# Swin-style block on one core: the first layer norm moved from channels on partitions to tokens on partitions

## The chip, the cores and the metric

One core of one Trainium2 chip. The metric is the device time of one execution in microseconds. Before the change the median of 3 runs is 596.34 us (595.48 to 596.77).

## What is computed

The input `x` is 32 images of 96 channels by 16 x 16 tokens, in float32. Two layers follow each other. Only the start of the first one is touched:

```python
x = x.transpose(0, 2, 3, 1)                       # tokens x 96 channels
mu = x.mean(-1, keepdims=True)                    # layer norm over the 96 channels of a token
var = ((x - mu) ** 2).mean(-1, keepdims=True)
xn = (x - mu) * rsqrt(var + 1e-5) * norm1_g + norm1_b
xs = roll(xn, (-4, -4))                           # windows of 8 x 8 tokens, 4 per image
q, k, v = split(xw @ qkv_w + qkv_b)               # 12 heads of 8 channels
attn = softmax(q @ k.T * SCALE + rel_bias + mask)
x = x + roll(attn @ v @ proj_w + proj_b, (4, 4))
x = x + gelu(layernorm2(x) @ fc1_w + fc1_b) @ fc2_w + fc2_b
```

The second layer (a layer norm over the whole image, depthwise convolutions, attention between channels) is not touched.

## The kernel before, in words

Three stages run one after the other: window attention with the first residual (`window_attention`), the MLP (`mlp`) and the channel attention. The whole activation lives in SBUF as `stream`, 96 channels on partitions by 32 x 256 tokens.

Window attention is written out by hand for each engine. Each engine has a function `step(t, ...)` that says in which order it does its parts of the work, and runs it for t = -3 to 32 (`led_image_loop`, L62). Engines take their instructions in order, so a wait of one instruction holds everything behind it on that engine. The work is software pipelined over images. Step t does the attention of image t, the projection of image t - 1, the second scores of t + 1, the q, k and v of image t + 2, and the first layer norm of image t + 3. An image has two pairs of windows, so most operations of the attention come twice a step (p = 0 and 1).

The first layer norm keeps channels on partitions. TensorE multiplies the image by the matrix `center` (`centre`, L517), ScalarE squares the result (L338), TensorE averages the squares with the matrix `average` (`spread`, L522), ScalarE makes the inverse deviation by a logarithm and an exponential (`inverse_deviation`, L344 and L347, 96 x 256 elements each), and VectorE multiplies while it puts the tokens into window order (`normalise`, L424, two instructions).

TensorE's order in a step (L590) is: turn the probabilities of (t, 0) (L561); project t - 1 (L588); scores of (t + 1, 1) (L551); weigh (t, 0) (L574); centre t + 3 (L517); turn (t, 1); turn the heads of (t, 0) (L583); q, k and v of t + 2 (L529, L531, L537); weigh (t, 1); spread t + 3 (L522); scores of (t + 2, 0); turn the heads of (t, 1). All are float32.

ScalarE's order (L384) is: copy_ot of (t - 1, 1) (L379); copy_turned (t, 0) (L374); exponent (t, 1) (L368); square t + 3; copy_turned (t, 1); copy_ot (t, 0); copy_q t + 2 (L354); exponent (t + 1, 0); copy_v t + 2 (L363, four instructions, which wait for weigh (t, 1)); inverse_deviation t + 3. VectorE's order (L468) is: residual t - 1 (L465); normalise t + 2; add_bias (t + 1, 1) (L441); weigh_heads (t, 0) (L456 and L459); find_peak (t + 1, 1) (L449); copy_k t + 2 (L430); weigh_heads (t, 1); add_bias and find_peak (t + 2, 0). GpSimd subtracts the peaks (L324).

Two waits tie ScalarE to TensorE at the end of a step:

```python
def project(t, par):
    pe.wait_ge(s["ot_copied"], (t + 1) * 2)          # copy_ot of image t, both pairs
    pe.wait_ge(s["v_copied"], up_to(t + 2) * 4)      # copy_v of image t + 2
```

SyncE's queue issues all loads: image 0, constants, images 1 to 3 (`LOADS`, L280 and L281, into `stream`), then images 4 to 31 as two large transfers, then 34 small loads of weights for the later stages (L296).

Of the kernel before, what the change touches and what calls it, by code (L numbers as in the profile page):

```python
# [21 lines left out]
N = H * W  # L22
# [24 lines left out]
LOADS = ((0, 1), (1, 1), (2, 1), (3, 1), (4, B - 4))  # L47
UNROLLED = 4
# [13 lines left out]
def led_image_loop(engine, step):  # L62

    step(-3, 1)
    step(-2, 0)
    step(-1, 1)
    image_loop(engine, lambda t, half, par: step(t, par), tail=2)
    step(B, 0)
# [119 lines left out]
def window_attention(nc, ctx, a, sem, stream, ident, center, average, w_late, weights_in, zeroed_final):  # L188
# [3 lines left out]
    def bank(name, count=1):  # L192
# [15 lines left out]
    squares = sb("squares", [C, N])  # L208
    log_var = sb("log_var", [C, N])
    eps = sb("eps", [C, 1])  # L210
    rstd = sb("rstd", [C, N])
# [17 lines left out]
    centred = ps_a[0:C, 0, 0:N]  # L229
    ps_var = ps_a[0:C, 0, N:2 * N]  # L230
# [8 lines left out]
    normalising_in = sem("normalising_in")  # L239
# [4 lines left out]
    pe_set = sem("pe_set")  # L244
    zeroed = sem("zeroed")
    x_landed = [sem(f"x_landed{k}") for k in range(len(LOADS))]
    s = {n: sem(n) for n in (
        "centred_ready", "squares_ready", "var_ready", "log_ready", "rstd_ready", "normed_ready",
# [4 lines left out]
    FIRST, SECOND = 7, 7  # L253
# [4 lines left out]
    @block.sync  # L258
    def _(sp):
        def column(name):  # L260
            return a[name].rearrange("(c a) -> c a", a=1)

        normalising = ((center[:, :], a["c_center"]), (average[:, :], a["c_average"]))
        first = ((w_in[:, :], a["L0_conv_qkv_w"]),
                 (cols[:, 0:1], column("L0_conv_norm1_g")), (cols[:, 1:2], column("L0_conv_norm1_b")),
                 *((cols[:, 2 + k:3 + k], a["L0_conv_qkv_b"][k * C:(k + 1) * C].rearrange("(c a) -> c a", a=1))
                   for k in range(3)),
                 (head_mask[:, :], a["c_head_mask"]))
        second = (*((shift_mask[WN * top:WN * (top + 1), left, :], a["c_shift_mask"][WN * left:WN * (left + 1), top])
                    for top in range(2) for left in range(2)), (ident[:, :], a["c_ident"]),  # L270
                  (w_proj[:, :], a["L0_conv_proj_w"]), (cols[:, 5:6], column("L0_conv_proj_b")))
        assert (len(first), len(second)) == (FIRST, SECOND)
        late = weight_loads(a, w_late)

        def load(k):

            t, count = LOADS[k]
            images = x[t:t + count].rearrange("b c h w -> c b (h w)")
            rows = stream[:, t * N:(t + count) * N].rearrange("p (b n) -> p b n", n=N)
            sp.dma_start(rows[:, :, 0:N - SS * W], images[:, :, SS * W:N]).then_inc(x_landed[k], 16)  # L280
            sp.dma_start(rows[:, :, N - SS * W:N], images[:, :, 0:SS * W]).then_inc(x_landed[k], 16)  # L281

        load(0)
        for dst, src in normalising:
            sp.dma_start(dst, src).then_inc(normalising_in, 16)
# [12 lines left out]

    @block.gpsimd
    def _(pool):  # L300


        table = a["L0_conv_rel_bias"]
# [7 lines left out]
        nc.gpsimd.memset(eps[:, :], EPS).then_inc(zeroed, 1)  # L311
        nc.gpsimd.memset(v_blocks[:, :, :, :, :, :, :], 0.0).then_inc(zeroed, 1)
        pool.wait_ge(zeroed, 2)
        for e in range(2):
            for par in range(2):
                nc.gpsimd.memset(v_blocks[64 * e:64 * e + 64, par, :, :, :, e, HD:VC], 1.0).then_inc(zeroed, 1)
        pool.wait_ge(zeroed, 6)
        nc.gpsimd.memset(w_late["final"][:, :], 0.0).then_inc(zeroed_final, 1)

        def subtract_peak(t, p, par):  # L320
            u = t * 2 + p
            pool.wait_ge(s["peak_ready"], u + 1)
            sc = scores[:, par, p, :].rearrange("p (h m) -> p h m", m=WN)
            nc.gpsimd.tensor_tensor(sc, sc, peak[:, par, p, :].unsqueeze(2).to_broadcast((128, HEADS, WN)),  # L324
                                    ALU.subtract).then_inc(s["shifted"], 1)

        def step(t, half, par):
            subtract_peak(t, 0, par)
            subtract_peak(t, 1, par)

        image_loop(pool, step)

    @block.scalar
    def _(act):
        def square(t):
            act.wait_ge(s["centred_ready"], t + 1)
            need(act, s["var_ready"], t)
            nc.scalar.activation(squares[:, :], centred, ACT.Square).then_inc(s["squares_ready"], 1)  # L338

        def inverse_deviation(t):  # L340

            act.wait_ge(s["var_ready"], t + 1)
            need(act, s["rstd_ready"], t)
            nc.scalar.activation(log_var[:, :], ps_var, ACT.Ln, bias=eps[:, 0:1]).then_inc(s["log_ready"], 1)  # L344
            act.wait_ge(s["log_ready"], t + 1)
            need(act, s["normed_ready"], t * PAIRS)
            nc.scalar.activation(rstd[:, :], log_var[:, :], ACT.Exp, scale=-0.5).then_inc(s["rstd_ready"], 1)  # L347

# [7 lines left out]
        def copy_v(t, par):  # L356
            act.wait_ge(s["v_ready"], t + 1)
# [24 lines left out]
        act.wait_ge(zeroed, 6)  # L382

        def step(t, par):  # L384
# [5 lines left out]
            if real(t + 3):  # L390
                square(t + 3)
# [15 lines left out]
    def _(dve):  # L407
# [12 lines left out]
        def normalise(t):  # L420
            dve.wait_ge(s["rstd_ready"], t + 1)
            need(dve, s["v_ready"], t)
            for p in range(PAIRS):
                nc.vector.tensor_tensor(window_rows(normed[:, p * 2 * WN:(p + 1) * 2 * WN], p), shifted(centred, p),  # L424
                                        shifted(rstd[:, :], p), ALU.mult).then_inc(s["normed_ready"], 1)
# [36 lines left out]
        def add_residual(t):  # L462
            dve.wait_ge(s["proj_ready"], t + 1)
# [4 lines left out]
        def step(t, par):  # L468
# [19 lines left out]
        nc.vector.tensor_scalar(w_qkv[:, :], w_in[:, :], cols[:, 0:1], None, ALU.mult).then_inc(set_up, 1)  # L488
# [5 lines left out]
        nc.vector.tensor_scalar(b_q[:, :], b_q[:, :], SCALE, None, ALU.mult).then_inc(set_up, 1)  # L494
        led_image_loop(dve, step)

    @block.tensor
    def _(pe):
# [13 lines left out]
        def centre(t):  # L512
            for k, (first, count) in enumerate(LOADS):
                if is_image(t, min(first, UNROLLED)):
                    pe.wait_ge(x_landed[k], 32)
            need(pe, s["normed_ready"], t * PAIRS)
            nc.tensor.matmul(centred, center[:, :], stream[:, bass.ds(t * N, N)],  # L517
                             start=True, stop=True).then_inc(s["centred_ready"], 1)

        def spread(t):  # L520
            pe.wait_ge(s["squares_ready"], t + 1)
            nc.tensor.matmul(ps_var, average[:, :], squares[:, :], start=True, stop=True).then_inc(s["var_ready"], 1)  # L522

        def make_q_and_k(t):
            if is_image(t, 0):
                pe.wait_ge(set_up, 1)
# [63 lines left out]
        def step(t, par):  # L590
            if real(t):
                turn(t, 0, par)
            if real(t - 1):
# [5 lines left out]
            if real(t + 3):  # L599
                centre(t + 3)  # L600
            if is_image(t, -3):
                fold_q_k_v()
            if real(t):
                turn(t, 1, par)
                turn_heads(t, 0)
            if real(t + 2):
# [4 lines left out]
            if real(t + 3):  # L611
                spread(t + 3)
# [7 lines left out]
        pe.wait_ge(normalising_in, 16 * 2)  # L620
# [660 lines left out]
```

## Time and profile before

| | |
|---|---|
| median of 3 runs | 596.34 us |
| the profiled execution's own time | 599.53 us |
| its span, first to last instruction | 597.8 us |
| TensorE (PE) busy | 548.4 us, 92% |
| VectorE (DVE) busy | 362.9 us, 61% |
| ScalarE (ACT) busy | 327.9 us, 55% |
| GpSimd (POOL) busy | 161.2 us, 27% |
| window attention / MLP / channel attention | up to about 289 / 405 / 598 us |

Times in the timeline are microseconds from the span's start. The span is cut from one profiled execution, 1.7 us shorter than that execution's own time, which in turn lies 3.2 us above the median. PE is TensorE's matmuls, PEld its weight loads, which overlap the matmuls. Matmul ends are modelled, so two neighbouring matmul groups can overlap by some tenths of a microsecond; distances from start to start are the firmer measure. One float32 matmul appears as two records, a transposition as one.

### The profile page before, as it was taken

The page shows a single profiled execution, that of the slowest core. Times are in us where ns is not written, and L with a number is a line of the kernel's source. Part 1 is how long each engine was busy: PE and PEld are TensorE (multiplying, and loading weights), DVE is VectorE, ACT ScalarE, POOL GpSimd, SP SyncE. Part 2 cuts the span into 40 slices and gives each one's busy share as a digit, 9 for nine tenths or more (in the row PEclk, how much of TensorE's full clock was granted, in tenths as well). Part 3 has the DMA queues.
Part 4 walks back from the last instruction along what each step waited for, and adds up shares of the span by engine and source line. Part 5 has one row for each costly group of instructions (what it writes and reads, how often), then busy time and mean ns, then how long its engine had stood idle before and what let it go on. Part 6 is the DMA issues. An engine that isn't in the chain of part 4 may idle for free. (4 is left out here: it accounts for less than half of the span.)

```text
span 597.8 us, 20839 instructions
## 1 busy us (share of the span) xinstructions
PE 548.4 (92%) x7900; PEld 327.6 (55%) x7900; DVE 362.9 (61%) x839; ACT 327.9 (55%) x749; POOL 161.2 (27%) x198
## 2 busy tenths in 40 slices
PE   2799999999999999998799999992899999999997
PEld 1466676666676666666333444441345555555563
DVE  0768778787778888787274333336325666655544
ACT  1367777777777777776499443332323444444432
POOL 7123333333333333333000000003322333333310
PEclk9999999999999999999799999996558999999999
DMA  4900000000000000000000000002432444444421
GB/s 86 206 7 3 1 0 0 0 0 0 0 0 0 0 0 0 0 0 2 2 0 0 0 0 0 0 0 49 108 87 78 115 111 114 113 115 115 125 63 29
DMA packets 28059, 22.87 MB, mean 38 GB/s; under 512 B 12280, under 2 KB 26744, under 8 KB 28024
## 3 DMA queue, kind: packets, MB, share of 16 engines
q1 hardware_dynamic: 24440, 16.66, 11.5%
q0 software_dynamic: 3584, 5.72, 4.2%
q8 instruction: 25, 0.41, 0.3%
q14 instruction: 10, 0.08, 0.1%
HBM read 15.22 MB, written 7.13 MB: 37 GB/s over the span
## 5 line engine op out<-in xcount | busy, mean ns | idle before, releaser
L324 POOL TENSOR_TENSOR scores<-scores,peak 128x768 f32<-128x768 f32 x64 | 94.3, 1474 | 174.0 <-DVE peak L449 174.0
L896 POOL DMA_DIRECT2D x_stack<-padded_x x96 | 52.3, 547 | 109.6 <-PE ps_v L1163 87.2
L441 DVE TENSOR_TENSOR scores<-ps_scores,bias 128x768 f32<-128x768 f32 x64 | 60.9, 951 | 25.0 <-PE ps_scores L551 25.0
L449 DVE TENSOR_REDUCE peak<-scores 128x12 f32<-128x768 f32 x64 | 60.7, 948 | 1.1
L574 PE MATMUL ps_out<-v_blocks,probs_t 128*64 128x54 f32 x1536 | 58.9, 227 | 2.1 <-ACT out_t L379 1.6
L574 PEld LDWEIGHTS ps_out<-v_blocks,probs_t 128*64 128x64 f32 x1536 | 50.6, 139 | 18.0 <-issue 15.2
L1163 PE MATMUL ps_qk<-x_stack,conv_w 40*32 40x256 f32 x1536 | 54.0, 411 | 5.5 <-ACT final_w L1009 5.5
L374 ACT COPY probs_t<-ps_probs 128x768 f32<-128x768 f32 x64 | 51.1, 798 | 13.4 <-PE ps_probs L561 13.4
L747 ACT ACTIVATE hidden<-ps_hidden,fc_b_folded 128x512 f32<-128x512 f32 x48 | 32.4, 688 | 42.9 <-PE ps_hidden L700 42.7
L430 DVE SCALAR_TENSOR_TENSOR k_blocks<-ps_scores,b_k,head_mask 96x1024 f32<-96x1024 f32 x32 | 41.0, 1280 | 23.5 <-PE ps_scores L531 23.5
L368 ACT ACTIVATE scores<-scores 128x768 f32<-128x768 f32 x64 | 54.1, 845 | 0.0
L1163 PE MATMUL ps_v<-x_stack,conv_w 40*32 40x256 f32 x1536 | 54.0, 411 | 0.0
L561 PE MATMUL ps_probs<-ident,scores 128*128 128x128 f32 x384 | 53.7, 277 | 0.0
L561 PEld LDWEIGHTS ps_probs<-ident,scores 128*128 128x128 f32 x384 | 45.5, 143 | 4.8 <-issue 1.0
L551 PE MATMUL ps_scores<-k_blocks,q_sb 32*64 32x256 f32 x768 | 45.0, 415 | 2.9 <-DVE scores L441 2.7
L782 DVE SCALAR_TENSOR_TENSOR mixed<-ps_y,fc_b,stream 96x384 f32 (+3 forms) x32 | 13.9, 476 | 54.1 <-PE ps_y L707 54.1
L338 ACT ACTIVATE squares<-ps_a 96x256 f32<-96x256 f32 x32 | 12.2, 381 | 60.9 <-PE ps_a L517 50.8
L700 PE MATMUL ps_hidden<-mixed,fc_scaled 96*128 (+1 forms) x96 | 43.7, 592 | 0.0
L707 PE MATMUL ps_y<-hidden,fc 128*96 128x512 f32 x96 | 43.7, 592 | 0.0
L1163 PEld LDWEIGHTS ps_qk<-x_stack,conv_w 40*32 40x32 f32 x1536 | 27.3, 112 | 28.3 <-issue 16.1
L981 ACT COPY qk_sb<-ps_qk 128x512 f32<-128x512 f32 x32 | 18.8, 586 | 40.1 <-PE ps_qk L1163 40.1
L363 ACT COPY v_blocks<-ps_b 64x96 f32<-64x96 f32 x128 | 30.7, 240 | 11.2 <-PE ps_out L574 7.3
(123 smaller groups left out, 857.2 us busy)
## 6 DMA issues: line engine op xcount, KB each, us to landing
x_stack<-padded_x SPq DMA_DIRECT2D x96, 54.0 KB
x_stack<-padded_x POOLq DMA_DIRECT2D x96, 54.0 KB, 2.7
padded_x<-x_pad SPq DMA_DIRECT2D x32, 121.5 KB, 2.5
out<-y_sb SPq DMA_DIRECT2D x32, 96.0 KB, 2.0
stream<-in_x SPq DMA_DIRECT2D x1, 2016.0 KB, 12.6
stream<-in_x SPq DMA_DIRECT2D x1, 672.0 KB, 16.0
rel_rows<-in_L_conv_rel_bias POOLq DMA_DIRECT2D x16, 24.0 KB, 2.4
stream<-in_x SPq DMA_DIRECT2D x4, 72.0 KB, 2.0
```

The source lines that it names most:

```text
L324: nc.gpsimd.tensor_tensor(sc, sc, peak[:, par, p, :].unsqueeze(2).to_broadcast((128, HEADS, WN)), ALU.subtract).then_inc(s["shifted"], 1)
L368: nc.scalar.activation(scores[:, par, p, :], scores[:, par, p, :], ACT.Exp).then_inc(s["probs_ready"], 1)
L374: nc.scalar.copy(probs_t[:, :], ps_turned).then_inc(s["turned_copied"], 1)
L441: nc.vector.tensor_tensor(scores[:, par, p, :].rearrange("p (g c) -> p g c", g=NG), ps_scores[:, :, 0:GROUP * WN], bias[:, p, :].rearrange ...
L449: nc.vector.tensor_reduce(peak[:, par, p, :], scores[:, par, p, :].rearrange("p (h m) -> p h m", m=WN), AX_X, ALU.max).then_inc(s["peak_re ...
L551: mm = nc.tensor.matmul(ps_scores[64 * w:64 * w + 64, g, 0:GROUP * WN], q, k, start=True, stop=True, skip_group_check=True)
L561: mm = nc.tensor.transpose(ps_turned[:, q * 128:(q + 1) * 128], scores[:, par, p, q * 128:(q + 1) * 128], ident[:, :])
L574: mm = nc.tensor.matmul(ps_out[64 * top:64 * top + 64, 0, q * 2 * VC:(q + 3) * 2 * VC], probs_t[:, q * 128 + 64 * top:q * 128 + 64 * top + ...
L700: nc.tensor.matmul(ps_hidden[:, par * HT + h, :], fc1[:, h * 128:(h + 1) * 128], mixed[:, bass.ds(k * CHUNK, CHUNK)], start=True, stop=Tru ...
L707: mm = nc.tensor.matmul(ps_y[0:C, par, :], w["fc2"][:, h, :], hidden[:, par, h, :], start=(h == 0), stop=(h == HT - 1))
L896: engine.dma_start(x_stack[64 * half + i * HC:64 * half + (i + 1) * HC, slot, :, :], rows).then_inc(landed[slot], 16)
L1163: mm = nc.tensor.matmul(ps[32 * k:32 * k + 32, r, :], conv_w[rows, kind, j, k, :], grid(x_stack[rows, slot, k, :], PADW)[:, :, j:j + W], s ...
```

## The change

The layer norm of image t + 3 is done with tokens on partitions. A step now holds: `turn_tokens`, two transpositions of an image half (96 x 128) into 128 tokens x 96 channels in PSUM; `measure`, two statistics instructions on VectorE (128 x 96 each), and `gather_spread`, two aggregations (128 x 6 to 128 x 2); `inverse_deviation`, the same logarithm and exponential over 128 x 2; `scale`, two ScalarE copies (128 x 96) with the inverse deviation as a per-partition scale; `turn_back`, two transpositions to channels x tokens, in the next step; `copy_normed`, two ScalarE copies into window order. The mean is no longer subtracted from the data: `center` is multiplied once into the weights (`fold_mean`). The images are loaded a second time, one by one, into a two-slot buffer `x_now`; `stream` is loaded whole by two transfers, and is first used by the residual.

Core of the diff:

```diff
@@ SyncE @@
-        load(0)
+        def load(t, par):
+            need(sp, s["tokens_ready"], t - 1)
+            image = x[bass.ds(t, 1)].rearrange("a c h w -> c (a h w)")
+            sp.dma_start(x_now[:, par, 0:N - SS * W], image[:, SS * W:N]).then_inc(x_now_in[par], 16)
+            sp.dma_start(x_now[:, par, N - SS * W:N], image[:, 0:SS * W]).then_inc(x_now_in[par], 16)
+        load(0, 0)
+        sp.dma_start(ident[:, :], a["c_ident"]).then_inc(turning_in, 16)
         for dst, src in first:
             sp.dma_start(dst, src).then_inc(consts_in, 16)
-        load(1)
+        load(1, 1)
         for dst, src in second:
             sp.dma_start(dst, src).then_inc(second_in, 16)
-        for k in range(2, len(LOADS)):
-            load(k)
+        load(2, 0)
+        load_stream()
+        load(3, 1)
         sp.wait_ge(zeroed_final, 1)
         for dst, src in late:
             sp.dma_start(dst, src).then_inc(weights_in, 16)
+        image_loop(sp, lambda t, half, par: load(t, par), lead=2, start=4)
@@ ScalarE @@
+        def scale(t):
+            act.wait_ge(s["rstd_ready"], t + 1)
+            need(act, s["turned_back"], t)
+            for h in range(2):
+                nc.scalar.activation(scaled[:, h, :], ps_tokens[:, h, :], ACT.Copy,
+                                     scale=rstd[:, h:h + 1]).then_inc(s["scaled_ready"], 1)
+        def copy_normed(t):
+            act.wait_ge(s["turned_back"], t + 1)
+            need(act, s["v_ready"], t)
+            for p in range(PAIRS):
+                nc.scalar.copy(window_rows(normed[:, p * 2 * WN:(p + 1) * 2 * WN], p),
+                               shifted(ps_scaled, p)).then_inc(s["normed_ready"], 1)
@@ ScalarE's step @@
                 exponent(t, 1, par)
-            if real(t + 3):
-                square(t + 3)
+            if real(t + 2):
+                copy_normed(t + 2)
...
                 exponent(t + 1, 0, 1 - par)
+            if real(t + 3):
+                inverse_deviation(t + 3)
+                scale(t + 3)
             if real(t + 2):
                 copy_v(t + 2, par)
-            if real(t + 3):
-                inverse_deviation(t + 3)
@@ VectorE's step @@
                 add_residual(t - 1)
-            if real(t + 2):
-                normalise(t + 2)
...
                 find_peak(t + 1, 1, 1 - par)
+            if real(t + 3):
+                measure(t + 3)
+            if real(t + 3):
+                await_stats(t + 3)
             if real(t + 2):
                 copy_k(t + 2)
+            if real(t + 3):
+                gather_spread()
             if real(t):
                 weigh_heads(t, 1)
@@ TensorE @@
+        def fold_mean():
+            pe.wait_ge(set_up, 1)
+            nc.tensor.matmul(ps_folded, center[:, :], w_gained[:, :], start=True, stop=True).then_inc(folded, 1)
+        def turn_tokens(t, half, par):
+            pe.wait_ge(x_now_in[par], (half + 1) * 32)
+            need(pe, s["scaled_ready"], t * 2)
             need(pe, s["normed_ready"], t * PAIRS)
+            for h in range(2):
+                mm = nc.tensor.transpose(ps_tokens[:, h, :], x_now[:, par, h * 128:(h + 1) * 128], ident[0:C, 0:C])
+            mm.then_inc(s["tokens_ready"], 1)
+        def turn_back(t):
+            pe.wait_ge(s["scaled_ready"], (t + 1) * 2)
+            for h in range(2):
+                mm = nc.tensor.transpose(ps_scaled[:, h * 128:(h + 1) * 128], scaled[:, h, :], ident[:, :])
+            mm.then_inc(s["turned_back"], 1)
@@ TensorE's step @@
                 turn(t, 0, par)
+            if real(t + 2):
+                turn_back(t + 2)
             if real(t - 1):
                 project(t - 1, 1 - par)
...
                 weigh(t, 0, par)
-            if real(t + 3):
-                centre(t + 3)
             if real(t):
                 turn(t, 1, par)
                 turn_heads(t, 0)
+            if real(t + 3):
+                turn_tokens(t + 3, half + 1 + par, 1 - par)
             if real(t + 2):
                 make_q_and_k(t + 2)
                 make_v(t + 2)
             if real(t):
                 weigh(t, 1, par)
-            if real(t + 3):
-                spread(t + 3)
             if real(t + 2):
                 score(t + 2, 0)
```

Besides, GpSimd sets `eps` before its loads of the bias table, ScalarE waits for that alone ahead of its first step and for the zeroed `v_blocks` only at its first copy_v, and the residual of image 0 waits for `stream`. VectorE copies the folded weights (96 x 288) out of PSUM ahead of its first step.

## Rows read from the trace of the kernel before

**Rows 1.** Waits over the whole span: total us, times, longest
```profile
PE ps_b L588 <- ACT out_t L379: 11.1, 30, 0.5
```

**Rows 2.** Timeline of one inner step: start us, us, engine, line, operation, idle before
```profile
120.23 0.67 PE L522 MATMUL ps_a<-squares,average 96*96 96x256 f32 x2
...
120.40 1.04 ACT L363 COPY v_blocks<-ps_b 64x96 f32<-64x96 f32 x4 [0.23 <-PE ps_out L574]
...
121.47 0.47 ACT L344 ACTIVATE log_var<-ps_a,eps 96x256 f32<-96x256 f32 x1
...
122.05 0.42 ACT L347 ACTIVATE rstd<-log_var 96x256 f32<-96x256 f32 x1
...
122.37 0.24 ACT L379 COPY out_t<-ps_out 96x128 f32<-96x128 f32 x1
...
122.75 0.67 PE L588 MATMUL ps_b<-out_t,w_proj 96*96 96x256 f32 x2 [0.34 <-ACT out_t L379]
...
123.95 0.91 PE L574 MATMUL ps_out<-v_blocks,probs_t 128*64 128x54 f32 x24
...
126.07 0.60 PE L529 MATMUL ps_scores<-normed,w_qkv 96*96 96x256 f32 x2
...
127.22 1.28 DVE L430 SCALAR_TENSOR_TENSOR k_blocks<-ps_scores,b_k,head_mask 96x1024 f32<-96x1024 f32 x1 [0.63 <-PE ps_scores L531]
```

**Rows 3.** Timeline, TensorE's projection of image 0 and of image 28
```profile
41.83 0.67 PE L588 MATMUL ps_b<-out_t,w_proj 96*96 96x256 f32 x2 [0.18 <-ACT out_t L379]
...
268.34 0.67 PE L588 MATMUL ps_b<-out_t,w_proj 96*96 96x256 f32 x2 [0.18 <-ACT out_t L379]
```

**Rows 4.** Timeline of step 29, which has no first layer norm in it
```profile
269.55 0.91 PE L574 MATMUL ps_out<-v_blocks,probs_t 128*64 128x54 f32 x24
...
270.39 0.87 PE L561 MATMUL ps_probs<-ident,scores 128*128 128x128 f32 x6
...
271.44 0.32 PE L583 MATMUL ps_out<-ident,heads_out 128*96 128x128 f32 x1 [0.17 <-DVE heads_out L459]
...
271.59 0.60 PE L529 MATMUL ps_scores<-normed,w_qkv 96*96 96x256 f32 x2
...
276.60 0.91 PE L574 MATMUL ps_out<-v_blocks,probs_t 128*64 128x54 f32 x24
```

**Rows 5.** Groups by line: busy us, mean ns of one, idle before
```profile
L786 DVE BATCH_NORM_STATS2 stats<-mixed (+1 forms) x32 | 12.0, 415 | 2.0 <-DVE mixed L782 1.0
...
L456 DVE RECIPROCAL recip<-ps_out 128x12 f32<-128x12 f32 x64 | 14.1, 221 | 4.8 <-PE ps_out L574 4.8
...
L990 ACT ACTIVATE logits<-logits 128x24 f32<-128x24 f32 x32 | 7.1, 223 | 8.6 <-DVE logits L1079 8.6
...
L379 ACT COPY out_t<-ps_out 96x128 f32<-96x128 f32 x64 | 16.5, 258 | 3.3 <-PE ps_out L583 3.2
```

**Rows 6.** Timeline of the start, TensorE and SyncE's queue
```profile
7.75 1.12 PE L503 MATMUL ps_out<-cols,w_in 96*96 96x1 f32 x6 [2.41 <-DMA head_mask<-in_c_head_mask]
...
13.39 4.30 SPq L281 DMA_DIRECT2D stream<-in_x  x1
...
16.41 1.06 PE L529 MATMUL ps_scores<-normed,w_qkv 96*96 96x256 f32 x2
...
17.74 8.40 SPq L296 DMA_DIRECT2D fc<-in_L_conv_fc_w  x2
...
37.93 3.23 SPq L296 DMA_DIRECT2D alpha<-in_L_conv_alpha  x8
...
45.16 0.60 PE L529 MATMUL ps_scores<-normed,w_qkv 96*96 96x256 f32 x2
```

**Rows 7.** Page, loads of one image: KB each, median us to landing
```profile
stream<-in_x SPq DMA_DIRECT2D x4, 72.0 KB, 2.0
```

**Rows 8.** Stretches: length, busy us of PE, PEld, DVE, ACT, POOL, granted clock
```profile
280.00:285.00 5.00, 3.56 (x51) 2.73 (x47) 1.46 (x5) 2.22 (x5) 0.83 (x1) 1.00 0.00 0
285.00:290.00 5.00, 2.49 (x28) 1.49 (x29) 1.39 (x4) 1.49 (x4) 0.10 (x1) 0.95 0.01 3
```

More of the change, by code:

```diff
@@ L62, in led_image_loop @@
 def led_image_loop(engine, step):
[L64 to L68, printed above, removed]
+    step(-3, -2, 1)
+    step(-2, -1, 0)
+    step(-1, -1, 1)
+    image_loop(engine, step, tail=2)
+    step(B, B // 2, 0)
 def image_loop(engine, step, tail=1, lead=1, between=None, start=0):
@@ L207, in window_attention @@
     b_proj = sb("b_proj", [C, 1])
[L208 to L211, printed above, removed]
+    w_gained = sb("w_gained", [C, 3 * C])
+    token_stats = sb("token_stats", [128, 2, 6])
+    spread = sb("spread", [128, 2, 2])
+    log_var = sb("log_var", [128, 2])
+    eps = sb("eps", [128, 1])
+    rstd = sb("rstd", [128, 2])
+    scaled = sb("scaled", [128, 2, C])
+    x_now = sb("x_now", [C, 2, N])
     normed = sb("normed", [C, N])
@@ L244, in window_attention @@
     pe_set = sem("pe_set")
+    folded = sem("folded")
+    centred = sem("centred")
     zeroed = sem("zeroed")
-    x_landed = [sem(f"x_landed{k}") for k in range(len(LOADS))]
+    x_now_in = [sem("x_now_in0"), sem("x_now_in1")]
+    stream_in = sem("stream_in")
     s = {n: sem(n) for n in (
-        "centred_ready", "squares_ready", "var_ready", "log_ready", "rstd_ready", "normed_ready",
+        "tokens_ready", "stats_ready", "spread_ready", "log_ready", "rstd_ready", "scaled_ready", "turned_back", "normed_ready",
         "q_ready", "k_ready", "q_copied", "k_copied", "v_ready", "v_copied",
@@ L261, in column @@
             return a[name].rearrange("(c a) -> c a", a=1)
-        normalising = ((center[:, :], a["c_center"]), (average[:, :], a["c_average"]))
-        first = ((w_in[:, :], a["L0_conv_qkv_w"]),
+        first = ((center[:, :], a["c_center"]), (w_in[:, :], a["L0_conv_qkv_w"]),
                  (cols[:, 0:1], column("L0_conv_norm1_g")), (cols[:, 1:2], column("L0_conv_norm1_b")),
@@ L269, in _ @@
         second = (*((shift_mask[WN * top:WN * (top + 1), left, :], a["c_shift_mask"][WN * left:WN * (left + 1), top])
-                    for top in range(2) for left in range(2)), (ident[:, :], a["c_ident"]),
+                    for top in range(2) for left in range(2)), (average[:, :], a["c_average"]),
                   (w_proj[:, :], a["L0_conv_proj_w"]), (cols[:, 5:6], column("L0_conv_proj_b")))
@@ L273, in _, with load_stream @@
         late = weight_loads(a, w_late)
[L275 to L281, printed above, removed]
-        load(0)
-        for dst, src in normalising:
-            sp.dma_start(dst, src).then_inc(normalising_in, 16)
+        def load(t, par):
[3 more added lines that the diff above has]
+            sp.dma_start(x_now[:, par, N - SS * W:N], image[:, 0:SS * W]).then_inc(x_now_in[par], 16)
+        def load_stream():
+            images = x.rearrange("b c h w -> c b (h w)")
+            rows = stream[:, :].rearrange("p (b n) -> p b n", n=N)
+            sp.dma_start(rows[:, :, 0:N - SS * W], images[:, :, SS * W:N]).then_inc(stream_in, 16)
+            sp.dma_start(rows[:, :, N - SS * W:N], images[:, :, 0:SS * W]).then_inc(stream_in, 16)
+        load(0, 0)
+        sp.dma_start(ident[:, :], a["c_ident"]).then_inc(turning_in, 16)
         for dst, src in first:
             sp.dma_start(dst, src).then_inc(consts_in, 16)
-        load(1)
+        load(1, 1)
         for dst, src in second:
             sp.dma_start(dst, src).then_inc(second_in, 16)
-        for k in range(2, len(LOADS)):
-            load(k)
+        load(2, 0)
+        load_stream()
+        load(3, 1)
         sp.wait_ge(zeroed_final, 1)
@@ L300, in _ @@
     def _(pool):
+        nc.gpsimd.memset(eps[:, :], EPS).then_inc(zeroed, 1)
         table = a["L0_conv_rel_bias"]
@@ L334, in _ @@
     def _(act):
[L335 to L338, printed above, removed]
         def inverse_deviation(t):
-            act.wait_ge(s["var_ready"], t + 1)
+            act.wait_ge(s["spread_ready"], (t + 1) * 2)
             need(act, s["rstd_ready"], t)
-            nc.scalar.activation(log_var[:, :], ps_var, ACT.Ln, bias=eps[:, 0:1]).then_inc(s["log_ready"], 1)
+            nc.scalar.activation(log_var[:, :], spread[:, :, 1], ACT.Ln, bias=eps[:, 0:1]).then_inc(s["log_ready"], 1)
             act.wait_ge(s["log_ready"], t + 1)
-            need(act, s["normed_ready"], t * PAIRS)
+            need(act, s["scaled_ready"], t * 2)
             nc.scalar.activation(rstd[:, :], log_var[:, :], ACT.Exp, scale=-0.5).then_inc(s["rstd_ready"], 1)
+        def scale(t):
[10 more added lines that the diff above has]
+                               shifted(ps_scaled, p)).then_inc(s["normed_ready"], 1)
         def copy_q(t):
@@ L381, in _, with step @@
         nc.scalar.preload_act_table_set("natural_log_exp_and_others")
-        act.wait_ge(zeroed, 6)
-        def step(t, par):
+        act.wait_ge(zeroed, 1)
+        def step(t, half, par):
             if real(t - 1):
@@ L418, in set_up_rest, with measure, await_stats, gather_spread @@
             dve.wait_ge(set_up, 8)
[L420 to L425, printed above, removed]
+        def measure(t):
+            dve.wait_ge(s["tokens_ready"], t + 1)
+            need(dve, s["spread_ready"], t * 2)
+            for h in range(2):
+                nc.vector.bn_stats(token_stats[:, h, :], ps_tokens[:, h, :]).then_inc(s["stats_ready"], 1)
+        def await_stats(t):
+            need(dve, s["log_ready"], t)
+            dve.wait_ge(s["stats_ready"], (t + 1) * 2)
+        def gather_spread():
+            for h in range(2):
+                nc.vector.bn_aggr(spread[:, h, :], token_stats[:, h, :]).then_inc(s["spread_ready"], 1)
         def copy_k(t):
@@ L466, in add_residual, with step @@
                                            op0=ALU.add, op1=ALU.add).then_inc(s["residual_done"], 1)
-        def step(t, par):
+        def step(t, half, par):
             if real(t - 1):
                 add_residual(t - 1)
-            if real(t + 2):
-                normalise(t + 2)
             if real(t + 1):
@@ L510, in fold_v @@
             nc.tensor.matmul(ps_out[0:C, 0, 0:1], w_proj[:, :], b_v[:, 0:1], start=True, stop=True).then_inc(pe_set, 1)
[L512 to L515, printed above, removed]
-            need(pe, s["normed_ready"], t * PAIRS)
[L517 to L522, printed above, removed]
+        def fold_mean():
[4 more added lines that the diff above has]
+            need(pe, s["scaled_ready"], t * 2)
+            need(pe, s["normed_ready"], t * PAIRS)
+            for h in range(2):
+                mm = nc.tensor.transpose(ps_tokens[:, h, :], x_now[:, par, h * 128:(h + 1) * 128], ident[0:C, 0:C])
+            mm.then_inc(s["tokens_ready"], 1)
+        def turn_back(t):
+            pe.wait_ge(s["scaled_ready"], (t + 1) * 2)
+            for h in range(2):
+                mm = nc.tensor.transpose(ps_scaled[:, h * 128:(h + 1) * 128], scaled[:, h, :], ident[:, :])
+            mm.then_inc(s["turned_back"], 1)
         def make_q_and_k(t):
             if is_image(t, 0):
-                pe.wait_ge(set_up, 1)
+                pe.wait_ge(centred, 1)
             pe.wait_ge(s["normed_ready"], (t + 1) * PAIRS)
@@ L588, in project, with step @@
             nc.tensor.matmul(ps_proj, w_proj[:, :], out_t[:, par, :], start=True, stop=True).then_inc(s["proj_ready"], 1)
-        def step(t, par):
+        def step(t, half, par):
             if real(t):
                 turn(t, 0, par)
+            if real(t + 2):
+                turn_back(t + 2)
             if real(t - 1):
```

27 lines of the change are left out of this document (16 added, 11 removed).

## The prediction

> **What bounds the kernel now.** I first read the table of busy times: TensorE is busy 92% of the span, the next engine 61%. Then I read the waits. In window attention only one wait of TensorE returns in almost every step: `project` waits for ScalarE's `out_t` (L379), 11.1 us in 30 times, or 0.37 us each [rows 1]. So TensorE sets the pace, and ScalarE's end of a step is already level with it. Any change that makes that end later moves the whole pace, because TensorE takes its work in order and everything of the next step stands behind `project`.
>
> The timeline of one step shows the ring that closes over the engines [rows 2]. I cut it at two points. **Part A**, from `project` (122.75) to the q matmul (126.07), is TensorE alone: 3.32 us. **Part B**, from q to the next `project`, goes over other engines: k is ready and copy_k starts 1.15 us after q (127.22), `weigh` lets copy_v start (120.40), four copies take 1.04, logarithm and exponential (121.47 and 122.05) follow, and only then copy_ot (122.37), 0.38 before `project`. The step is 8.09 us long: (268.34 - 41.83) / 28 [rows 3]. So Part B is 4.77.
>
> Step 29 is the control that the trace gives for free: it has no first layer norm in it and takes 7.05 us, from 269.55 to 276.60 [rows 4]. The old norm costs 1.04 us a step. The question is whether the new one costs less in the same ring.
>
> **TensorE's own work.** Removed per step are two matmuls of 96 x 256. `spread` takes 0.60 from start to start (120.23 to the scores at 120.83; the group itself lasts 0.67 [rows 2]), `centre` much the same. Added are four transpositions. Six of them plus what follows take 271.44 - 270.39 = 1.05, less 0.17 of waiting, so 0.88, or 0.15 each; where their weight loads are hidden they cost a little less, and I take 0.11, so 0.22 for two, between nothing and 0.29 [rows 4]. TensorE alone would gain about 8.09 - 7.05 - 0.44 = 0.60 us a step.
>
> **Part A after.** `project` to `weigh` 1.20 [rows 2]; then `weigh` to `turn` 0.84, `turn` 0.88, heads to q 0.15 [rows 4], `turn_tokens` 0.22. That is 3.29; the wait for the heads of 0.17 [rows 4] shrinks as `normalise` leaves VectorE ahead of them, and I keep 0.06: 3.35. `centre` pays for `turn_tokens` and no more. VectorE's statistics stand behind find_peak, where it waited 0.63 us for k [rows 2]. A statistics instruction takes 415 ns for 256 elements [rows 5]; 96 elements lie between the small operations' 0.22 and that. Two fit into the 0.63 or overrun it by up to 0.2; I take nothing.
>
> **Part B after.** This is where the change moves a chain. The inverse deviation and `scale` now stand *ahead of* copy_v, and they wait for `gather_spread`, which stands *behind* copy_k. Before, copy_v started right when `weigh` ended, and the norm's two activations stood behind it. `project` waits for both copy_v and copy_ot. From q on:
> - copy_k starts at 1.15 and lasts 1.28 [rows 2]: 2.43.
> - two aggregations: nothing like them is in the trace. Nearest in size is the reciprocal of 128 x 12, 221 ns; the statistics row is 415 [rows 5]. Small instructions partly overlap, so I take 0.30 for both; ends 0.15 and 0.83.
> - three handoffs at 0.10 (logarithm end 121.94 to exponential 122.05 is 0.11 [rows 2]): 0.30; from 0.24 to 0.33.
> - logarithm and exponential over two elements: the small activation of 128 x 24 takes 223 ns [rows 5]. I take 0.22 each; ends 0.18 each (a little under that row, as there are fewer elements) and the old 0.47 and 0.42 [rows 2].
> - `scale`, two of 128 x 96 out of PSUM: copy_ot's 96 x 128 takes 258 ns, and copy_v's four run at 0.26 each [rows 2, 5]. I take 0.52; ends 0.44 and twice 0.42.
> - copy_v 1.04 and copy_ot to `project` 0.38 [rows 2].
>
> Sum: 2.43 + 0.30 + 0.30 + 0.44 + 0.52 + 1.04 + 0.38 = 5.41, where it was 4.77. ScalarE itself is free earlier (q copy and exponent end about 2.3 after q), so it stands waiting for VectorE. All high ends together would make Part B 2.43 + 0.83 + 0.33 + 0.89 + 0.84 + 1.42 = 6.74 and the time 56 us longer, but they are rows of 256 elements for work on 2 to 96, so I let the range reach only part of the way. The step becomes 3.35 + 5.41 = 8.76, **0.67 longer**. The new chain works in the 28 steps between the projections of image 0 and image 28: +18.8 us. TensorE then idles about 1.3 us a step.
>
> The Trainium skill (ScalarE: Activation LUTs, section "What ACT_TABLE_LOAD costs") says that each per-partition pointer operand of an activation adds about 93 ns, over a fixed cost of 186 ns. The two `scale` and the logarithm have such an operand. The trace agrees in direction: the logarithm with its pointer bias takes 0.05 more than the exponential. By the Trainium skill's figures the chain would be an estimated 0.15 longer, and the time some 4 us more.
>
> GpSimd and `copy_normed` cost nothing: `copy_normed` takes two copies of 258 ns where the square stood, on an engine that idles 45% of the span; without that cover it would cost 0.5 a step. turn_back stands in TensorE's wait ahead of `project` (0.34 in the step shown [rows 2], about 1 us now). If that wait were gone, it would cost 0.22.
>
> **Start.** Three effects. (1) The q of image 0 begins at 16.41 [rows 6]. Now, from the end of the bias matmuls at 8.87: fold 1.2, copy out 0.4, statistics 0.5, aggregation 0.3, two activations 0.5, `scale` 0.5, turn_back and turn_tokens at the low clock 0.5 each, copy_normed 0.5, handoffs 0.6: 14.4. That is 2.0 earlier, of which I keep 1.4 by step 0, since the aggregation of image 1 stands ahead of the bias table on VectorE. (2) SyncE's queue is blocked by the large transfers from 13.39 to 26.14, and the late loads end at 41.16 [rows 6]. `stream` is now 32 images and not 28, one more single image stands behind it, and it starts two issues earlier: 12.75 x 32/28 is +1.8, two issues more and two less cancel, so the late loads end near 43. Only then is image 4 issued (0.9 for two), and it lands 2.0 us later [rows 7]: 46. `turn_tokens` of image 4 is due just before the q at 45.16 [rows 6], less the lead: 43.6. TensorE stalls some 2.4 us once; from 0 to 4. (3) Later images are issued two steps ahead of their use and are hidden. Start in sum: -1.4 + 2.4 - 0.3 (the stall covers one step's extra chain) = +0.7. Stages two and three do not change.
>
> **Sum:** 18.8 + 0.7 = +19.5 us. The profiled execution's own 599.53 would become 619.0; put onto the median 596.34, which is what I forecast: **615.8 us**.
>
> **Rivals.**
> 1. *Not slower: the chain from aggregation to `scale` is short enough.* It decides at the same place: B may be at most 8.09 - 3.29 = 4.80, so aggregation, handoffs, activations and `scale` together at most 0.95. My low ends sum to 0.15 + 0.24 + 0.36 + 0.44 = 1.19, a step of 8.33, +6.7 us. Below 0.95 TensorE's own gain begins to show; at its best 0.60 x 28 = 17 us faster, 579. For it: I have no row for an aggregation, and small operations overlap. Against it: three dependent handoffs and six instructions, none of which the rows show under 0.15. Chance 0.10, split between about 0.2% and faster.
> 2. *The clock falls.* TensorE's granted clock stays 1.00 with 3.56 of 5 us busy (280 to 285) and falls with 2.49 of 5 (285 to 290) [rows 8]. After the change it is busy about 7.4 of 8.76, so it should hold. If it went to the lower level in all steps, TensorE's 3.35 of Part A and the 1.15 ahead of copy_k would nearly double: +3.5 us a step, near 710. One drop after the stall at image 4 would cost about 3 us, which is in the range. The Trainium skill (TensorE: Matmul & The Clock Gate, section "Part 4: PE-mode transpose") says that transpositions do not count as activity in the same way; with two matmuls turned into four transpositions that speaks against this change. Chance 0.03.
> 3. *The late load dominates.* If the weights' issues push image 4 later than I think and the following images with it, a stall of up to 10 us once: 625. Chance 0.05.
> 4. *The small operations are dear* (aggregation 0.4 each, `scale` 0.35 each): 0.5 + 0.2 more a step, near 635. Chance 0.07.
>
> My forecast, a step of 8.45 to 9.0, has 0.75. About 0.2% (1.2 us) is what a measurement of this kernel can tell from no change. The range runs from the low ends with a good start (603) to the dear ScalarE figures with a longer stall (627). Chances: faster 0.06, same 0.03, slower 0.91.
>
> **What would show it.** Right: `project` waits for `out_t` about 1 us a step; a wait of the logarithm for VectorE's aggregation (about 0.5 a step) appears; copy_v no longer waits for `weigh`; scores (t + 2, 0) wait for copy_k; the distance of projections is 8.7 to 8.8; one wait of `turn_tokens` for a load near 44 us. Wrong: a distance at or under 8.09, TensorE without a wait ahead of `project`, or a granted clock under 1.00 between 60 and 260 us.

## The result, and the profile after

The changed kernel takes 609.37 us (median of 4 runs, 606.66 to 616.0; the ratio leaves out the 616.0, a run in the slower state) against 596.22 us for the kernel before in the same comparison. The ratio is 1.0204, with a 95% interval of 1.0178 to 1.023: slower by about 2%, and clear of no change. The forecast was 615.8 us in a range of 603 to 627. The profiled execution's own time is 608.33 us, its span 606.6.

TensorE does less than before, yet the kernel is slower. On the page of the changed kernel, busy time, share and instructions of TensorE:

```profile
PE 536.4 (88%) x7902; PEld 322.1 (53%) x7902; DVE 369.7 (61%) x904; ACT 332.8 (55%) x845; POOL 161.1 (27%) x198
```

Two of the changed kernel's waits from 60 to 220 us (19 steps of each), with total us, times and longest:

```profile
ACT log_var L350 <- DVE spread L458: 14.6, 19, 0.8
...
PE ps_b L636 <- ACT out_t L401: 11.8, 19, 0.8
```

The first is new: ScalarE's logarithm waits 0.77 us in every step for VectorE's aggregation. The second answers to [rows 1]: TensorE's wait ahead of `project` is now 0.62 us a step (11.8 / 19), where it was 0.37.

The timeline around the projection at 122.57, which comes 8.34 us after the one before it, and the start of the next step. It answers to [rows 2]; the idle time before an instruction and what ended it stand in brackets:

```profile
119.84 0.23 DVE L458 BATCH_NORM_AGGREGATE spread<-token_stats 128x2 f32<-128x6 f32 x2
...
120.11 0.30 ACT L350 ACTIVATE log_var<-spread,eps 128x2 f32<-128x2 f32 x1 [0.75 <-DVE spread L458]
...
120.44 0.20 ACT L353 ACTIVATE rstd<-log_var 128x2 f32<-128x2 f32 x1
...
120.67 0.57 ACT L359 ACTIVATE scaled<-ps_a,rstd 128x96 f32<-128x96 f32 x2
...
121.13 1.03 ACT L385 COPY v_blocks<-ps_b 64x96 f32<-64x96 f32 x4
...
122.18 0.26 ACT L401 COPY out_t<-ps_out 96x128 f32<-96x128 f32 x1
...
122.57 0.67 PE L636 MATMUL ps_b<-out_t,w_proj 96*96 96x256 f32 x2 [0.39 <-ACT out_t L401]
...
125.86 0.60 PE L577 MATMUL ps_scores<-normed,w_qkv 96*96 96x256 f32 x2
...
127.09 1.28 DVE L463 SCALAR_TENSOR_TENSOR k_blocks<-ps_scores,b_k,head_mask 96x1024 f32<-96x1024 f32 x1 [0.48 <-PE ps_scores L579]
...
128.29 0.23 DVE L458 BATCH_NORM_AGGREGATE spread<-token_stats 128x2 f32<-128x6 f32 x2
```

Read upwards from `project` (122.57): copy_ot, copy_v, `scale`, exponential, logarithm, aggregation follow each other with no gap over 0.13 us. The aggregation starts as copy_k ends: copy_k of that step runs from 118.64 to 119.92, that of the next from 127.09 to 128.37. Part A is 125.86 - 122.57 = 3.29, where it was 3.32.

The distances of projections tell where the time went:

| between projections of | before | after | difference |
|---|---|---|---|
| start to image 0 | 41.83 | 39.25 | -2.58 |
| image 0 to 2 | 16.03 | 24.39 | +8.36 |
| image 2 to 28 | 210.48 (26 x 8.10) | 218.88 (26 x 8.42) | +8.40 |
| image 28 to the MLP's first table load | 21.03 | 21.09 | +0.06 |

So window attention ends 14.2 us later, 8.4 of them between images 2 and 28 and 5.8 up to image 2. At the start stands one wait of TensorE, on the changed kernel's list of waits:

```profile
PE ps_a L563 <- DMA x_now<-in_x: 4.4, 1, 4.4
```

and the stretches around it, with the granted clock third from the end:

```profile
42.00:46.00 4.00, 0.37 (x3) 0.12 (x1) 0.86 (x2) 0.96 (x2) 1.47 (x1) 1.00 0.08 19
46.00:50.00 4.00, 3.27 (x15) 2.57 (x16) 1.21 (x3) 1.20 (x2) 0.00 (x0) 0.50 0.23 57
```

TensorE stands still from 42.4 to 46.7, because image 4 is loaded behind the 34 weights, and then works at the lower clock level until 56 us. In the kernel before the clock was 1.00 there.

The whole span grew by 8.8 us only: the MLP takes 0.8 us longer in this profile, and the third stage is 6.2 us shorter (191.5 to 185.3). Nothing in either was changed; the last two experiments are about that.

### The profile page after: what moved, and what is told of

The parts are those of the page before. It is cut to its first block and busy times, and to the rows that moved or that the text cites. A ratio compares the mean times of both kernels' runs of the same rounds, so it can differ in the third digit from the quotient of the medians.

```text
span 606.6 us, 21295 instructions
## 1 busy us (share of the span) xinstructions
PE 536.4 (88%) x7902; PEld 322.1 (53%) x7902; DVE 369.7 (61%) x904; ACT 332.8 (55%) x845; POOL 161.1 (27%) x198
## 5 line engine op out<-in xcount | busy, mean ns | idle before, releaser
L609 PE MATMUL ps_probs<-ident,scores 128*128 128x128 f32 x384 | 55.9, 283 | 2.2 <-issue 2.2
L1212 PE MATMUL ps_qk<-x_stack,conv_w 40*32 40x256 f32 x1536 | 52.1, 399 | 5.5 <-ACT final_w L1058 5.5
L599 PE MATMUL ps_scores<-k_blocks,q_sb 32*64 32x256 f32 x768 | 46.1, 422 | 11.9 <-issue 8.7
L1212 PE MATMUL ps_v<-x_stack,conv_w 40*32 40x256 f32 x1536 | 52.4, 395 | 0.0
L609 PEld LDWEIGHTS ps_probs<-ident,scores 128*128 128x128 f32 x384 | 42.9, 143 | 6.9 <-issue 4.9
L636 PE MATMUL ps_b<-out_t,w_proj 96*96 96x256 f32 x64 | 22.0, 426 | 17.7 <-ACT out_t L401 17.7
L1126 DVE TENSOR_REDUCE peak<-ps_gram 128x2 f32<-128x24 f32 x32 | 5.9, 183 | 45.1 <-PE ps_gram L1238 45.1
```

Source lines behind the costliest of these rows:

```text
L599: mm = nc.tensor.matmul(ps_scores[64 * w:64 * w + 64, g, 0:GROUP * WN], q, k, start=True, stop=True, skip_group_check=True)
L609: mm = nc.tensor.transpose(ps_turned[:, q * 128:(q + 1) * 128], scores[:, par, p, q * 128:(q + 1) * 128], ident[:, :])
L1212: mm = nc.tensor.matmul(ps[32 * k:32 * k + 32, r, :], conv_w[rows, kind, j, k, :], grid(x_stack[rows, slot, k, :], PADW)[:, :, j:j + W], s ...
```

## The experiments

**One part of the change in the old kernel: the order alone.** In the kernel before, the logarithm and the exponential move ahead of copy_v:

```diff
+            if real(t + 3):
+                inverse_deviation(t + 3)
             if real(t + 2):
                 copy_v(t + 2, par)
-            if real(t + 3):
-                inverse_deviation(t + 3)
```

`make_v` also waits for the earlier copy_v, which that order no longer implies.

> The kernel before, with one thing of the change alone: ScalarE's logarithm and exponential stand ahead of copy_v and not behind it (and v waits for the copy of the v before it, which has long been made). Theory (the place in ScalarE's order is the price, not the new operations): the two wait for the averaged squares, copy_v starts about 1.6 us later, project about 0.6 us later, the distance of projections goes from 8.1 to about 8.7, and the time to about 612. Rival (the order is free, as ScalarE idles 45% of the span): 596 within 2 us.

Measured: 614.16 us in one run, 17 us more than the 597.12 for the kernel before in the same job. The distance of projections is 8.59 us in every step. In its timeline the logarithm waits for the averaged squares and copy_v stands behind both:

```profile
124.81 0.47 ACT L344 ACTIVATE log_var<-ps_a,eps 96x256 f32<-96x256 f32 x1 [0.77 <-PE ps_a L522]
125.40 0.42 ACT L347 ACTIVATE rstd<-log_var 96x256 f32<-96x256 f32 x1
125.72 1.02 ACT L363 COPY v_blocks<-ps_b 64x96 f32<-64x96 f32 x4
126.77 0.26 ACT L379 COPY out_t<-ps_out 96x128 f32<-96x128 f32 x1
```

copy_v starts 1.61 us after `spread` (124.11), where it started 0.17 after it. The exchange cost 13.7 us in the 28 steps (28 x 8.58 against 28 x 8.09), on an engine that idles 45% of the span. The other 3 us of the 17 lie outside the steps; the third stage, where nothing was changed, took 191.8 us in this profile. The chain theory stands, and the rival that the order is free falls.

**The loads of images 4 and 5 ahead of the weights,** in the changed kernel:

```diff
         load(3, 1)
+        load(4, 0)
+        load(5, 1)
         sp.wait_ge(zeroed_final, 1)
         for dst, src in late:
             sp.dma_start(dst, src).then_inc(weights_in, 16)
-        image_loop(sp, lambda t, half, par: load(t, par), lead=2, start=4)
+        image_loop(sp, lambda t, half, par: load(t, par), lead=3, start=6)
```

> The changed kernel with the single images 4 and 5 issued ahead of the 34 late weight loads; nothing else differs. Theory (the late load of image 4 stalls TensorE for 4.35 us at 42.4 us, and the idle time drops TensorE's clock to the lower level until about 56 us): the wait of the token transposition for its load is gone, the granted clock is 1.00 from 40 to 55 us, the projections of image 0 and image 2 lie 16.8 us apart and not 24.4, and the time falls by 7 to 8 us, to about 601; the distance of later projections stays 8.34 and 8.53 in turn. Rival (the loads run against something else, and the weights pushed back delay a later stage): the stall moves elsewhere, and the time stays within 2 us of 609.

Measured: 605.19 us (603.08 to 605.86), ratio to before 1.0119 (1.0061 to 1.0178). The stall and the low stretch are gone, against the rival, and images 0 and 2 lie 16.84 us apart. The gain is 4 us (5 by the ratios, 1.0204 to 1.0119) and not 7 to 8, because the projection of image 0 itself comes 2.2 us later (41.42). The q of image 1 (24.48) still came 0.1 us earlier than in the changed kernel (24.61); what came later is TensorE's first rise from the lower level. The same six transpositions, in the changed kernel and here:

```profile
33.10 0.87 PE L609 MATMUL ps_probs<-ident,scores 128*128 128x128 f32 x6
...
33.57 1.54 PE L611 MATMUL ps_probs<-ident,scores 128*128 128x128 f32 x6
```

The granted clock reads 1.00 in both stretches, so this is told from the durations alone. Why it rose later was not tried. The end of window attention moves from 303.6 to 297.9.

**The aggregation ahead of copy_k.** The aggregations must wait for the statistics. A tiny instruction ahead of them, here called the carrier, carries that wait:

```diff
+            if real(t + 3):
+                nc.vector.tensor_tensor(carrier[:, :], eps[:, :], eps[:, :], ALU.mult)
+                gather_spread()
             if real(t + 2):
                 copy_k(t + 2)
-            if real(t + 3):
-                gather_spread()
```

VectorE also waits once, ahead of its first step, until `eps` is set; that line and the carrier's allocation are not shown.

> The changed kernel with the two aggregations ahead of copy_k on VectorE instead of behind it, with one tiny multiplication ahead of them that carries the wait for the statistics. Theory (the chain copy_k, aggregation, logarithm, exponential, scale, copy_v, copy_ot sets the distance of projections): ScalarE's logarithm starts when the exponential of the scores ends, some 0.75 us earlier, its wait for the aggregation is gone, and the distance falls from 8.43 to 7.6 to 7.8; 26 undisturbed steps give 16 to 21 us, so about 590, under the kernel before. Rival (TensorE's four transpositions and their exposed weight loads are what costs): the distance stays over 8.3 and the time within 3 us of 609. The stall at image 4 stays in both.

Measured: 612.39 us (608.43 to 614.57), ratio 1.0226 (1.0156 to 1.0295). No gain; the distances are 8.25 and 8.59 in turn. By what was expected this spoke for the rival. With the loads moved too:

> Both edits together. Theory: the gains add up, since one lies at the start and one in the steps: no stall, a distance of 7.6 to 7.8, and a time of about 582, 2 to 3% under the kernel before. Rival (without the longer steps the loads or ScalarE bind again): less than two thirds of the sum, so over 588.

Measured: 605.27 us (602.27 to 607.86), as with the loads alone. Its timeline shows why the edit had not done what it was meant to do:

```profile
120.49 1.47 POOL L338 TENSOR_TENSOR scores<-scores,peak 128x768 f32<-128x768 f32 x1 [1.24 <-DVE peak L485]
...
120.78 1.20 DVE L520 TENSOR_TENSOR carrier<-eps 128x1 f32<-128x1 f32 x1
...
121.90 0.24 DVE L461 BATCH_NORM_AGGREGATE spread<-token_stats 128x2 f32<-128x6 f32 x2
...
122.06 1.24 DVE L466 SCALAR_TENSOR_TENSOR k_blocks<-ps_scores,b_k,head_mask 96x1024 f32<-96x1024 f32 x1
...
123.41 0.68 PE L604 MATMUL ps_scores<-k_blocks,q_sb 32*64 32x256 f32 x12 [1.12 <-issue]
```

The carrier, one element per partition, lasts 1.20 us and ends at 121.98; GpSimd's subtraction ends at 121.96. Over the run the carrier's shortest is 0.158 us and its median 1.195. It pushed copy_k from 1.23 us behind q (127.09 - 125.86) to 2.06 (122.06 - 120.00), and everything behind copy_k with it: TensorE now stands 1.12 us ahead of the scores, which start 0.11 us after copy_k ends. The edit had shortened one wait (the logarithm's, from 0.75 us to 0.26) and made another on the same ring.

These two runs show one thing more. The granted clock fell in the midst of the steps, once in the first one's profile (images 16 to 18 lie 9.36 and 9.11 us apart) and twice in the second's (9.23 and 9.18, 9.25 and 9.18). It read 0.57 from 64 to 68 and from 166 to 170 us of the second. Each fall cost 1.6 us. TensorE was busy for 138 of the 160 us from 60 to 220, against 141 in the changed kernel, where the clock did not fall.

So I changed the carrier. The wait for `eps`, which it no longer reads, goes too:

```diff
-                nc.vector.tensor_tensor(carrier[:, :], eps[:, :], eps[:, :], ALU.mult)
+                nc.vector.tensor_reduce(carrier[:, :], token_stats[:, 0, 0:2], AX_X, ALU.max)
```

> As e2_gather_first, but the instruction that carries the wait is a reduction of two elements of the statistics, with one SBUF input, and not a multiplication with two SBUF inputs. In e2 and e3 that multiplication of 128 x 1 took 1.20 us in the steps and 0.16 where GpSimd was idle, and it ended when GpSimd's subtraction ended. Theory (the chain theory stands, and the carrier was held by GpSimd's subtraction, so that copy_k started 1.0 us late): the carrier takes under 0.25 us, copy_k starts 1.1 us after q, the distance of projections falls to 7.6 to 7.8, and the time to about 590. Rival (the place of the aggregation gains nothing, as TensorE's own work bounds the step): the distance stays at 8.2 to 8.5 and the time over 606.

Measured: 588.19 us (584.4 to 589.42), ratio 0.9845 (0.9782 to 0.9908), faster than the kernel before by 1.6%, clear of no change. The carrier takes 0.155 us. The distances behind image 2 are 7.57 and 7.68 in turn, while images 0 and 1 still lie 15.17 us apart, over the stall. With the loads:

> As e5_gather_carrier2, with images 4 and 5 issued ahead of the late weights as in e1_loads_first. Theory: no stall at image 4, clock 1.00 from 40 us on, a distance of 7.6 to 7.8, and a time of 582 to 587, under the kernel before by 2%. Rival (as above): the time stays at 603 to 606 as in e3_both.

Measured: 580.59 us (579.5 to 581.29), ratio to the kernel before 0.9727 (0.9677 to 0.9778), 5% under the changed kernel, and 1.4 us below what was expected. The distance of projections is 7.57 and 7.68 in turn. Its timeline:

```profile
120.39 0.15 DVE L520 TENSOR_REDUCE carrier<-token_stats 128x1 f32<-128x2 f32 x1
120.46 0.24 DVE L461 BATCH_NORM_AGGREGATE spread<-token_stats 128x2 f32<-128x6 f32 x2
...
120.61 0.83 ACT L393 ACTIVATE scores<-scores 128x768 f32<-128x768 f32 x1
120.67 1.28 DVE L466 SCALAR_TENSOR_TENSOR k_blocks<-ps_scores,b_k,head_mask 96x1024 f32<-96x1024 f32 x1
...
121.35 0.28 ACT L353 ACTIVATE log_var<-spread,eps 128x2 f32<-128x2 f32 x1
...
122.36 1.02 ACT L388 COPY v_blocks<-ps_b 64x96 f32<-64x96 f32 x4
...
123.82 0.38 PE L573 MATMUL ps_a<-ident,scaled 128*96 128x128 f32 x2
...
124.04 0.60 PE L640 MATMUL ps_b<-out_t,w_proj 96*96 96x256 f32 x2
```

The logarithm starts right behind the exponential of the scores (L393), with no wait, and `project` follows turn_back (L573) without one. From 60 to 220 us TensorE is busy for 96% of the time at the full clock. The stretch of the combined version, with its length, PE's busy time and, third from the end, the granted clock:

```profile
60.00:220.00 160.00, 153.96 (x2101) 111.57 (x2100) 144.21 (x316) 126.80 (x358) 61.70 (x43) 1.00 0.05 13
```

The same stretch of the changed kernel, where it is busy for 88%:

```profile
60.00:220.00 160.00, 141.35 (x1900) 100.57 (x1896) 128.09 (x267) 115.48 (x324) 55.58 (x39) 1.00 0.05 12
```

Both versions with the second carrier beat both kernels, this one by more. With the aggregations in their new place a step takes 7.63 us, less than the 8.10 of the kernel before: the longer steps came from where two of the new operations stood, and not from the operations themselves.

**The third stage.** Both kernels were profiled once more, unchanged.

> The kernel before, unchanged, profiled once more. In its first profile TensorE's clock was at the lower level from about 408 to 453 us, 45 us, and the third stage took 191.5 us; in the changed kernel's it was 31 us and 185.3. Theory (the end of the low stretch does not depend on the kernel but on when it falls in time): a second profile of the same kernel gives another length of the stretch, and the third stage is shorter by about half the difference. Rival (the stretch belongs to the kernel): 45 us and 191.5 again, within 1 us.

> The changed kernel, unchanged, profiled once more. Both theories of the steps: 8.34 and 8.53 in turn, and one wait of the token transposition of image 4 for its load of 4.2 to 4.5 us. Theory (the low stretch of the third stage varies from run to run): its length is not 31 us again, and the third stage takes half of the difference longer than 185.3. Rival: 31 us and 185.3 again.

| profile | third stage | TensorE at the low level in it | span |
|---|---|---|---|
| before | 191.5 us | 44.4 us | 597.8 |
| before, again | 187.5 us | 37.6 us | 594.2 |
| after | 185.3 us | 30.7 us | 606.6 |
| after, again | 187.3 us | 37.5 us | 608.4 |

The times are 596.0 and 610.11 us. The stage is counted from ScalarE's table load at its start, the low level from stretches of 2 us. With the low stretch alike (37.6 and 37.5) the stage takes the same in both kernels (187.5 and 187.3). The rival, that the stretch belongs to the kernel, falls: the 6 us that the first pair of profiles showed as a gift of the change are chance. That the stage shortens by half of what the low stretch does holds only roughly: 6.8 us less of it gave 4.0 us in the kernel before and 2.0 in the changed one, where 3.4 was expected. Between the second pair the spans differ by 14.2 us. The wait for image 4's load was 4.3 us again, the distances 8.34 and 8.52. What sets the end of the low stretch was not tried.

## Why the prediction was right, and where its sizes were off

**What bounds and the ring: right.** The wait of the logarithm for the aggregation, copy_v behind `scale`, and `project` waiting longer for `out_t` all stand in the timeline. The exchange of two instructions in the old kernel (+13.7 us in its steps) and the aggregation ahead of copy_k in the new one (609.4 to 588.2) show it from both sides. Three of the signs did not come as told: the distances are 8.34 and 8.53 and not 8.7 to 8.8, `project` waits 0.62 us a step and not about 1, and the scores' wait for copy_k appears as TensorE's own issue (0.22 and 0.33 ahead of L599), not under copy_k's name.

**Part A: right.** Forecast 3.35, measured 3.29. Two transpositions cost what the matmul `centre` had cost.

**Part B: mis-sized.** Forecast 5.41; the measured mean is 8.43 - 3.29 = 5.14. The forecast of the step, 8.76, was 0.33 too long, so the steps cost 8.4 us (26 of them at 0.32) and not the 18.8 of 28 at 0.67. By terms, in the step that ends at 122.57: from the start of the aggregations to `project` 122.57 - 119.84 = 2.73, where I had 5.41 - 2.43 = 2.98. The aggregations take 0.23 (I had 0.30). Logarithm and exponential take 0.30 and 0.20 (0.22 each). `scale` takes 0.57 (0.52), but copy_v starts 0.11 before it ends, an overlap that I had left out between different instructions. The aggregations hand over in 0.04 and the exponential in 0.03 (0.10 each); logarithm to exponential is 0.03, too. In that step copy_k also ended about 0.1 sooner after q than the 2.43 that I took from one row. The handoffs are the largest of these, 0.10 for three where I had 0.30 and a low end of 0.24; the activations were dearer than I had them, by 0.11. From the start of the aggregations to copy_v it was 1.29 us, between my low ends (1.19) and my middle values (1.56).

The pointer operand showed itself. The two-element logarithm has a pointer bias and takes 296 ns on average, the exponential has none and takes 203. The Trainium skill (ScalarE: Activation LUTs, section "What ACT_TABLE_LOAD costs") gives about 93 ns for such an operand, and the trace agrees.

**TensorE's own gain: right in kind.** Forecast 0.60 us a step if nothing else bound; the combined version, where ScalarE no longer binds, gives 8.10 - 7.63 = 0.47, with 0.2 us of waiting ahead of the scores still in each step.

**Start: mis-sized, by 5 us.** Forecast +0.7, measured 8.36 - 2.58 = +5.8. The lead came larger than I kept (2.6, not 1.4). The q of image 0 starts at 14.31, 2.10 us earlier (I had 2.0); the rest, up to the projection, goes with the earlier rise of TensorE from the lower level, and in the run with the loads moved, where it rose later, the projection leads by 0.4 only. The stall of image 4 was foreseen by place and cause, but at 2.4 us; it was 4.4, since the weights' issues ended at 44.1 and not near 43, and the transposition was due at 42.4 and not 43.6. And the fall of the clock after it, which I had named and put into the range at about 3 us, came in all four profiles that had the stall, and belonged into the sum. It accounts for what the 8.36 holds beyond the stall and the longer steps: 8.36 - 4.35 - 0.64 = 3.4. The run with the loads moved gives 24.39 - 16.84 = 7.55 for stall and clock together, so 3.2 for the clock.

**Rivals.** "Not slower" put its break-even at 0.95 us from the aggregation to the end of `scale`. With the overlap it was 121.13 - 119.84 = 1.29. "The clock falls in all steps" did not happen: 1.00 from 60 to 220 us with TensorE 88% busy there (141.35 of 160). "The late load dominates" came in part: stall and clock cost 7.6 us, but by image 4 alone. "The small operations are dear" did not come: the two aggregations took 0.23 together and not 0.8, the two `scale` 0.57 and not 0.70. The Trainium skill's rule that transpositions do not count in the same way as activity (TensorE: Matmul & The Clock Gate, section "Part 4: PE-mode transpose") spoke for a lower clock in the steps. With four more transpositions and two fewer matmuls a step the clock held in the changed kernel. It fell for about 4 us at a time, once and twice, only in the two runs in which TensorE also waited 1.1 us a step for copy_k; whether the transpositions had a part in that is not shown.

The sum came out 6 us too high: 10 too much in the steps, 5 too little at the start, and about 1 in the rest. That the two large errors had opposite signs and half cancelled is luck; the direction is not, since the steps alone cost 8.4 us.

## What to carry to other kernels

When a small chain is moved ahead of a copy that frees the next matmul, price the place before the operations: the logarithm over 2 elements instead of 256 saved about 0.2 us, and its new place cost more. Ask of each wait what stands ahead of it on the *releasing* engine; the place of the aggregation in VectorE's order, behind copy_k or ahead of it, was worth 21 us here (609.37 to 588.19). When loads move behind a queue of small ones, take their landing time seriously: here the idle time was paid twice, once as a wait (4.4 us) and once at the low clock (3.2 us).

## What the runs showed of the hardware that I had not expected

A VectorE multiplication of one element per partition with both inputs in SBUF lasts 1.20 us while GpSimd subtracts over 128 x 768 in SBUF, and 0.16 us in the two cases where GpSimd did not subtract (at 11.00 us it was clearing a tile, at 15.00 it was idle); in the step shown it ended 0.02 us after GpSimd's instruction. A reduction with one SBUF input in the same place takes 0.154 to 0.156 us in all 32 cases. The Trainium skill (SBUF — State Buffer, section "Who interferes with whom") says that a VectorE instruction with two SBUF inputs contends with a GpSimd instruction that reads SBUF, and not with one that only writes it. The trace agrees on both, 1.20 us against 0.16; I had not looked for it in a carrier of one element. The difference between the two carriers is 24 us of the kernel's time (612.39 to 588.19).

The stretch in which TensorE stays at the lower level after the second transition between stages was 37.6 and 44.4 us in two profiles of the same kernel, though TensorE was busy without a gap for most of it. In the changed kernel it was 30.7 and 37.5. A profile of this kernel therefore carries an uncertainty of 2 to 4 us that has nothing to do with what was changed.
